# Dividing the softmax weights on GpSimd before the product with the values, one core

## The reference

```python
q, k, v = split(shift_token(x) @ wqkv)          # 128 -> 3 * 512
q, k = l2norm(q) * qs, l2norm(k) * ksc          # per head
q, k = rotary_xpos(q, k)
sim  = einsum('bhwid,bhwjd->bhwij', q * 8, look_around(k))   # own window and the one before
attn = softmax(where(mask, -max, sim))
out  = einsum('bhwij,bhwjd->bhwid', attn, look_around(v))
x    = x + out @ wo
x    = x + (a * gelu(g)) @ w2 + b2              # a, g from layernorm(shift_token(x)) @ w1
```

## Time and profile before

| | |
|---|---|
| median of 3 runs | 974.99 us (973.52 to 976.41) |
| the profiled execution | 971.3 us, of which the profiled span is 969.5 us |
| PE busy | 862.3 us (89%) |
| ACT busy | 701.7 us (72%) |
| DVE busy | 634.5 us (65%) |
| POOL busy | 631.0 us (65%) |
| mean granted PE clock | 0.983 of full speed |

### The profile page before, as it was taken

How to read it: one execution, slowest core, us unless ns; L and a number is a source line. 1 busy time by engine, 2 the same in 40 slices (tenths; PEclk the granted TensorE clock), 3 DMA queues, 4 the chain that set the end, 5 groups by cost and what they waited for, 6 DMA issues and landing times.

```text
span 969.5 us, 26414 instructions
## 1 busy us (share of the span) xinstructions
PE 862.3 (89%) x10836; PEld 580.5 (60%) x10836; DVE 634.5 (65%) x1082; ACT 701.7 (72%) x1449; POOL 631.0 (65%) x500
## 2 busy tenths in 40 slices
PE   0678889989899898998999989999999999999876
PEld 0345666666667666666566656565656565656552
DVE  5874666666667567576575776757575758575632
ACT  0446786977868779677797778787878787878651
POOL 4588677675876758667586665757575758585700
PEclk9979999999999999999999999999999999999997
DMA  9100000000000000000000000000000000000000
GB/s 295 30 1 3 1 2 2 3 3 2 2 3 1 3 1 1 3 2 3 1 2 3 1 2 2 1 21 4 17 7 23 2 23 2 21 3 24 1 23 11
DMA packets 20482, 13.47 MB, mean 14 GB/s; under 512 B 4579, under 2 KB 19597, under 8 KB 20237
## 3 DMA queue, kind: packets, MB, share of 16 engines
q1 hardware_dynamic: 15108, 10.49, 3.6%
q10 hardware_dynamic: 5256, 1.31, 0.7%
HBM read 9.70 MB, written 2.10 MB: 12 GB/s over the span
## 4 chain that ended last, share of the span: by engine, by line
PE 63%; ACT 15%; DVE 10%; issue 7%; POOL 3%; DMA 1%; DVEq 0%; POOLq 0%; SPq 0%; ACTq 0%
PE pQK L1181 8%; PE pS L1108 6%; PE pT L1093 5%; PE pT L1050 5%; PE pM L1125 5%; PE pV L1146 4%; PE pS L1082 4%; PE pM L1254 4%; DVE m L734 4%; PE pT L1237 3%; PE pQK L1345 3%; PE pM L1119 2%; PE pS L1069 2%; ACT prT L545 2%; ACT pr L598 1%
## 5 line engine op out<-in xcount | busy, mean ns | idle before, releaser
L366 POOL TENSOR_TENSOR rn<-rn,half_neg 128x16 f32<-128x16 f32 x64 | 187.5, 2929 | 5.3
L379 POOL TENSOR_TENSOR m<-m 128x1024 f32<-128x1024 f32 x64 | 150.9, 2358 | 0.0
L364 POOL TENSOR_SCALAR rn<-ss 128x16 f32<-128x16 f32 x64 | 16.3, 254 | 193.3 <-DVE ss L747 192.1
L386 POOL TENSOR_TENSOR qkn<-m,rn 128x1024 f32<-128x1024 f32 x64 | 121.7, 1902 | 5.0
L1181 PE MATMUL pQK<-wqkv,hT 128*128 128x512 f32 x256 | 123.6, 606 | 0.9 <-DVE m L734 0.9
L780 DVE TENSOR_REDUCE mx<-pS 128x8 f32<-128x1024 f32 x64 | 78.1, 1220 | 63.8 <-PE pS L1082 63.8
L561 ACT ACTIVATE sq<-pQK 128x1024 f32<-128x1024 f32 x64 | 65.4, 1022 | 25.5 <-PE pQK L1181 25.4
L747 DVE TENSOR_REDUCE ss<-sq 128x16 f32<-128x1024 f32 x64 | 77.6, 1213 | 6.7 <-ACT sq L561 6.4
L782 DVE TENSOR_TENSOR pr<-pS,mx 128x1024 f32<-128x1024 f32 x64 | 78.4, 1225 | 2.2
L521 ACT ACTIVATE kT<-pT 128x512 f32<-128x512 f32 x64 | 38.0, 595 | 57.3 <-PE pT L1050 56.8
L545 ACT ACTIVATE prT<-pT 128x1024 f32<-128x1024 f32 x64 | 65.0, 1016 | 15.6 <-PE pT L1093 14.8
(11 more groups left out here) (169 smaller groups left out, 2015.9 us busy)
## 6 DMA issues: line engine op xcount, KB each, us to landing
x<-in_L_attn_x SPq DMA_DIRECT2D x4, 512.0 KB, 9.4
xs<-in_L_attn_x SPq DMA_DIRECT2D x8, 256.0 KB, 2.8
out<-aqkT SPq DMA_DIRECT2D x8, 256.0 KB, 2.2
wqkv<-in_L_ffn_wqkv SPq DMA_DIRECT2D x2, 768.0 KB, 9.8
tab<-in_k_tab SPq DMA_DIRECT2D x1, 1024.0 KB, 10.4
w<-in_L_ffn_w SPq DMA_DIRECT2D x2, 341.0 KB, 10.5
wo<-in_L_ffn_wo SPq DMA_DIRECT2D x2, 256.0 KB
cst<-in_k_cst ACTq DMA_DIRECT2D x1, 404.5 KB, 4.3
```

The source lines that it names most:

```text
L366: eng.tensor_tensor(rn[:, k % 2, :], rn[:, k % 2, :], half_neg[:, 0:2 * H], ALU.pow).then_inc(S["rn_done"], 1)
L379: eng.tensor_tensor(m1[:, k % 2, :], m1[:, k % 2, :], m2[:, :], ALU.add).then_inc(S["add_done"], 1)
L386: eng.tensor_tensor(qkn[:, k % 2, :].rearrange("p (h d) -> p h d", d=DH), m1[:, k % 2, :].rearrange("p (h d) -> p h d", d=DH), rn[:, k % 2 ...
```

## The change

Each row of `pr` is summed on DVE after the exponential (`dve_totals`, a reduction over 128 x 1024 elements and a reciprocal of 128 x 8), and POOL multiplies the whole of `pr` with the reciprocals (`pool_weights`, 128 x 1024 elements). PE waits for that before it transposes the weights. `pe_values` then swaps its operands: the values are the stationary side and the transposed weights move, so that the output comes out already transposed, in `pS` for batch 0 and in `pM` for the others, and ACT evicts it directly to `oT`. The transposes of `o`, `dve_output` and the columns of ones are gone. `pe_values` of a batch runs one slot later than before (batch 0 at the end of slot 3). ACT's two carry copies become two DMAs a slot on SP's queue (`sp_carry`), with `vmix` in two buffers. `act_exp` moves ahead of the square. `qkn` becomes the same buffer as `m1`, `sm` moves to the buffer of `gg`, and the last transposes of a tile move from `pM` to `pV`.

```diff
+        def sp_carry(sp, step, b):
+            n, ct = count(step, b), step_count(step)
+            if not is_start(step):
+                need(sp, carried[b], 16 * (ct - 1))
+                sp.wait_ge(LS["s_mm"], n - 3)
+                sp.dma_start(kT[b][:, :, P:P + WIN], kT[b][:, :, WIN:P]).then_inc(carried[b], 16)
+            need(sp, kept[b], 16 * ct)
+            need(sp, LS["o_mm"], n - 3)
+            sp.wait_ge(LS["v_ev"], 2 * n + 2)
+            sp.dma_start(vmix[(ct + 1) % 2][b][64:P, :, :], vown[b][64:P, :, :]).then_inc(kept[b], 16)
...
                 pool_retention_norm(eng, new[1], 0)
                 return
+            turned = at(new, old, k - 2)
+            if turned:
+                pool_weights(eng, turned[1], turned[2])
             if old and k == NB - 1:
                 pool_ln(eng, old)
...
+        def pool_weights(eng, b, n):
+            eng.wait_ge(LS["rec_done"], n + 1)
+            eng.tensor_tensor(pr[:, b % 2, :, :], pr[:, b % 2, :, :],
+                              rec[:, b % 2, :].unsqueeze(2).broadcast_to([P, H, P]), ALU.mult).then_inc(LS["pn_done"], 1)
...
                 pool_mask_qk(eng, t, b)
                 if b + 2 < NB:
                     pool_retention_norm(eng, t, b + 2)
+            pool_weights(eng, 1, count((0, t), 1))
             if old:
                 pool_ln(eng, old)
...
+            if old and k > 0:
+                act_output(eng, old, k)
             if new:
-                if not is_start(new):
-                    need(eng, S["o_mm"], n - 3)
-                    eng.activation(vmix[k][64:P, :, 0:DH], vown[k][64:P, :, 0:DH], ACT.Copy).then_inc(S["v_kept"], 1)
-                    eng.activation(kT[k][:, :, P:P + WIN], kT[k][:, :, WIN:P], ACT.Copy).then_inc(S["carried"], 1)
...
-            if k == 0 and turned:
+            if turned and not (k == NB - 1 and new and new[0] == 0):
                 act_exp(eng, b, m)
...
-            else:
-                if old and k == NB - 1:
-                    act_shift_residual(eng, old)
-                if k > 0 and turned:
-                    act_exp(eng, b, m)
+            elif old and k == NB - 1:
+                act_shift_residual(eng, old)
...
-        def dve_output(eng, n):
+        def dve_totals(eng, b, n):
             S = LS
-            po = pS[:, :].rearrange("p (g z) -> p g z", g=2)[:, :, 0:4 * (DH + 1)].rearrange("p g (h d) -> p g h d", h=4)
-            eng.wait_ge(S["o_mm"], n + 1)
-            eng.reciprocal(rec[:, :, :], po[:, :, :, DH]).then_inc(S["rec_done"], 1)
-            eng.wait_ge(S["rec_done"], n + 1)
-            eng.tensor_tensor(o[:, :].rearrange("p (c g d) -> p g c d", g=2, d=DH), po[:, :, :, 0:DH],
-                              rec[:, :, :].unsqueeze(3).broadcast_to([P, 2, 4, DH]), ALU.mult).then_inc(S["o_done"], 1)
+            eng.wait_ge(S["exp_done"], n + 1)
+            eng.tensor_reduce(tot[:, :], pr[:, b % 2, :, :], AX.X, ALU.add).then_inc(S["tot_done"], 1)
+            eng.wait_ge(S["tot_done"], n + 1)
+            need(eng, S["pn_done"], n - 1)
+            eng.reciprocal(rec[:, b % 2, :], tot[:, :]).then_inc(S["rec_done"], 1)
...
             if k > 0 and old and not retain:
                 dve_residual(eng, old, k)
-            weighted = at(new, old, k - 3)
+            if turned and not retain:
+                dve_totals(eng, turned[1], turned[2])
...
                 if k + 2 < NB:
                     dve_retention_qk(eng, t, k + 2)
+                if k == 1:
+                    dve_totals(eng, 1, count((0, t), 1))
...
         def pe_turn_weights(eng, b, n, turned):
             S = LS
-            eng.wait_ge(S["exp_done"], n + 1)
+            eng.wait_ge(S["pn_done"], n + 1)
...
-            for i in range(H):
-                g, j = i // 4, i % 4
+            keys = (vmix[step_count(step) % 2][b], vown[b])
+            for j in range(4):
                 for w in range(2):
-                    col0 = g * 512 + j * (DH + 1)
-                    mm = eng.matmul(pS[64 * w:64 * w + 64, col0:col0 + DH + 1], prT[:, i, 64 * w:64 * w + 64],
-                                    (vown if w else vmix)[b][:, 2 * j + g, :], start=(j == 0), stop=True,
-                                    skip_group_check=True)
+                    for g in range(2):
+                        mm = eng.matmul(pooled(b)[64 * g:64 * g + 64, j * P + 64 * w:j * P + 64 * w + 64],
+                                        keys[w][:, 2 * j + g, :], prT[:, 4 * g + j, 64 * w:64 * w + 64],
+                                        start=True, stop=True, skip_group_check=True)
             mm.then_inc(S["o_mm"], 1)
...
+            if old and k > 0:
+                pe_values(eng, old, k, count(old, k), ff)
             if new:
                 l, n = new[0], count(new, k)
                 eng.wait_ge(S["h_ready"], 2 * n + 2)
                 need(eng, S["v_ev"], 2 * n)
+                if k == 2 and block_ffn:
+                    eng.wait_ge(G["osb"], ff[1] + 1)
...
-                pe_turn_output(eng, count(old, k))
+                pe_wo(eng, old[0], count(old, k))
...
-                    pe_ffn_out(eng, ff, lambda: weighted and pe_values(eng, weighted[1], weighted[2], turned))
+                    pe_ffn_out(eng, ff, first_wo)
...
+            if k == NB - 1 and new:
+                pe_values(eng, new, 0, count(new, 0))
```

More of the change, by code:

```diff
@@ L167, in program @@
         kT = [sb(f"kT{b}", [P, 4, P + WIN]) for b in range(NB)]
-        vown = [sb(f"vown{b}", [P, H, DH + 1]) for b in range(NB)]
-        vmix = [sb(f"vmix{b}", [P, H, DH + 1]) for b in range(NB)]
+        vown = [sb(f"vown{b}", [P, H, DH]) for b in range(NB)]
+        vmix = [[sb(f"vmix{u}_{b}", [P, H, DH]) for b in range(NB)] for u in range(2)]
         mx = sb("mx", [P, H])
@@ L318, in _, with body @@
                 sp.dma_start(w2[0:CHUNKS[2][1], l, 2, :], a["L0_ffn_w2"][l, 2 * P:HID, :]).then_inc(w_ld, 16)
[L320 to L327, removed]
+            def body(new, old, ff):
+                last = ff and ff[0] == 1
+                if last:
+                    need(sp, G["out"], 16 * ff[1])
+                    sp.dma_start(xs[:, :, :], x_steps[ff[1]]).then_inc(G["xs"], 16)
+                for k in range(NB):
+                    if new:
+                        sp_carry(sp, new, k)
+                if last:
+                    sp.wait_ge(G["osb"], ff[1] + 1)
+                    sp.dma_start(out_steps[ff[1]], osb[:, :, :]).then_inc(G["out"], 16)
+            run_bodies(sp, body)
+            for b in range(NB):
+                sp.wait_ge(kept[b], 16 * 2 * NT)
+                sp.wait_ge(carried[b], 16 * (2 * NT - 1))
             sp.wait_ge(G["out"], 16 * NT)
@@ L515, in act_slot @@
             turned = at(new, old, k - 2)
+            if old and k == 0 and old[0] == 1:
+                act_output(eng, old, 0)
             if turned:
@@ L533, in act_slot @@
                 eng.wait_ge(S["v_mm"], n + 1)
-                if not is_start(new):
-                    eng.wait_ge(S["v_kept"], n - 3)
+                need(eng, kept[k], 16 * step_count(new))
                 values = pV[:, :].rearrange("p (h d) -> p h d", h=H)
-                eng.activation(vown[k][:, :, 0:DH], values, ACT.Copy).then_inc(S["v_ev"], 1)
-                eng.activation(vmix[k][0:64, :, 0:DH], values[0:64], ACT.Copy).then_inc(S["v_ev"], 1)
+                eng.activation(vown[k][:, :, :], values, ACT.Copy).then_inc(S["v_ev"], 1)
+                eng.activation(vmix[step_count(new) % 2][k][0:64, :, :], values[0:64], ACT.Copy).then_inc(S["v_ev"], 1)
             if k == 1 and block_tile(ff) is not None:
@@ L600, in act_output @@
         def act_output(eng, step, b):
[L602 to L605, removed]
+            n = count(step, b)
+            eng.wait_ge(LS["o_mm"], n + 1)
+            need(eng, LS["wo_mm"], n)
+            eng.activation(oT[:, :, :], pooled(b)[:, 0:512].rearrange("p (c n) -> p c n", c=4),
+                           ACT.Copy).then_inc(LS["ot_ev"], 1)
         def act_gelu(eng, step, k):
@@ L765, in dve_rotate @@
             sum_squares()
-            if weighted:
-                dve_output(eng, weighted[2])
+            if final is not None:
+                dve_final(eng, final)
             if k == NB - 1 and l == 1 and normed:
@@ L823, in dve_slot @@
                 dve_hidden(eng, ff, 2)
-                if weighted:
-                    dve_output(eng, weighted[2])
                 dve_ffn_out(eng, ff)
             elif new:
-                dve_rotate(eng, new, k, weighted, normed=old)
-            elif weighted:
-                dve_output(eng, weighted[2])
+                dve_rotate(eng, new, k, normed=old, final=final)
+            elif final is not None:
+                dve_final(eng, final)
             if k == 0 and old:
@@ L1055, in pe_scores @@
             S = LS
-            evicted, subtracted, weighed = (counted(eng, v) for v in (2 * n + 2, n, n - 1))
             eng.wait_ge(mask_done, 1)
```

(10 more changed lines are left out.)

100 lines of the change are left out of this document (44 added, 56 removed).

## The result

The changed kernel takes 1015.55 us (median of four runs, 1013.55 to 1028.14) against 974.47 us for the kernel before on the same chip: ratio 1.0446, 95% interval 1.036 to 1.0532. The profiled execution took 1013.55 us (span 1011.7), 42.2 us more than before, where the sum of the prediction had 31.6. The spread of 15 us is new as well; the longest run had the lowest granted TensorE clock (0.953; the other three 0.965 to 0.972).

What follows compares the result with a forecast made beforehand. It took PE's transposes waiting for POOL's scaling two slots earlier as the loop that matters, POOL's longer round setting slots 1 to 3. Terms 21 + 3.2 + 3.2 + 2.2 + 2 = 31.6 on 971.3, plus 3.7: 1007 us, range 978 to 1035.

Steps and rivals of the forecast that it cites:

- PE and POOL as resources: Busy times expected in the changed profile: POOL near 753 us, PE near 834 us.
- POOL's multiplication, 1.90 us: New multiplication of 128 x 1024 by a broadcast operand in each slot, taken at 1.90 us, upper bound 2.36.
- Layer 0, slots 1 to 3, 18.65 us: From the start of slot 1, POOL's first round ends and slot 3 can start at 18.65 us; before, 16.35.
- that sign of being wrong: Prediction is wrong if DVE's new wait for the exponential makes PE's q and k projection wait for the rotation.
- PE ready for slot 3 at 15.5 us: Layer 0: with 7.75 us of work a slot, PE would be ready for slot 3 at 15.5 us after slot 1 starts.
- Retention, 2.9 us late and +1.3 us for the sum: Layer 0: PE enters the retention stretch 2.9 us late; DVE's uncovered sum for batch 1 adds 1.3 us.
- The rival that the lateness is taken up in the retention stretch: The 2.9 us are lost again among the retention stretch's waits: 987 us, 977 with the sum covered; 14%.
- The step of layer 0, +3.0 us: Layer 0 step: +2.9 lateness, +1.3 sum, -1.2 in slot 0, so +3.0 us, seven times: 21.
- The step of layer 1, +0.45 us: Layer 1 step: slot 3 waiting for POOL +0.85, layer-norm transposes +1.1, slot 0 -1.5, so +0.45 us, seven times: 3.2.
- The first steps and the drain: First step of layer 0 +3.2 us, first step of layer 1 +2.2 us, last batch in the drain +2 us.
- The whole: All terms over the whole kernel add up to 31.6 us more than the profiled execution before, 971.3 us.
- The carries, 0: 128 carries by DMA, issued about a slot ahead and due two slots (16 us) later, cost 0.

Runs made afterwards that it cites:

- a3_fill: Changed kernel with 20 transposes of a constant on PE ahead of its wait for POOL's scaling, in slot 3 only: 1005.74 us, 1.0343.
- b2_extra_wait: Kernel before with three idle POOL products (2.00 us together) at the new multiplication's place, waiting for the slot's exponential: 1003.31 us, 1.0329.
- b1_extra: Kernel before with three idle POOL products (2.00 us together) at the new multiplication's place, waiting for nothing: 981.77 us, 1.0104.
- a14_tiny_both: Changed kernel with POOL's multiplication cut to one column of 128 per head and DVE's sum taken over every eighth column: 983.6 us, 1.0119.
- a1_tiny: Changed kernel with POOL's multiplication cut to one column of 128 per head, its waits kept: 999.43 us, 1.0271.
- a8_fill_tot: Changed kernel with the edits of a2_totmove and a3_fill together: 996.6 us, 1.0244.
- a2_totmove: Changed kernel with DVE's sum for batch 1 in the retention stretch moved one piece later: 1007.07 us, 1.0367.
- c1_dma: Kernel before with only the two carries made by DMA on SP's queue, single value buffer kept: 965.46 us, 0.9936.
- a5_actcarry: Changed kernel with both carries made by ACT copies again instead of DMAs: 1022.78 us, 1.0525.
- a9_tiny_order: a1_tiny with, in slots 1 to 3, DVE's sum behind the sum of squares and POOL's short multiplication behind its maximum and power: 1022.01 us, 1.0522.

## Why the prediction was right, and where its sizes were off

The direction, the cause and the range held; the time came out 8.6 us above the 1007 us. By its own steps (the lengths of steps are taken from one POOL round of slot 1 to the next):

- *PE and POOL as resources.* POOL 749.4 us against my 753 held. PE had 847.3 against 834, because it works at half clock for longer: in a3_fill it is busy 869.0 us, of which the added transposes are 16 times 2.35, which leaves some 831 (an estimate).
- *POOL's multiplication, 1.90 us.* Measured 1.90. By the Trainium skill (GPSIMD Engine Reference, section 3.1) a two-input addition of 2048 fp32 elements measured 4497 ns on this engine; half of that, 2.25 us, is an estimate for 1024. It is near the addition here, 2.36 us, and not this form.
- *Layer 0, slots 1 to 3, 18.65 us.* Measured 19.06. The start of the maximum was 4.44 into the slot instead of 4.10, the multiplication 9.58 instead of 9.2; rounds without idleness came as said, and the wait of 3.21 us for POOL's scaling too. PE waited 2.3 us in the whole run for the rotation ahead of the q and k projection (0.9 before), so that sign of being wrong did not appear. b2_extra_wait shows the mechanism made alone, b1_extra that load is its smaller part.
- *PE ready for slot 3 at 15.5 us.* This would need slots of 7.75 us. PE's pieces of slot 1 in a14_tiny_both add up to 8.0 us without a gap, because the product with the values took 1.15 us (said 1.08) and the projection of v 1.05 (0.86 before), so that more than half of the 0.44 us of transposes that went came back. The maxima of a1_tiny are 8.3 us apart. None of this entered the sum, as POOL was later still, but it is why the short multiplication gave back only 17 us.
- *Retention, 2.9 us late and +1.3 us for the sum.* DVE's first product came at 29.6 us (said 29.1). In a3_fill PE's first retention product is 335.50 - 305.14 = 30.4 us after the start of slot 1, 3.5 us later than before, and the rest of the step is 0.4 us shorter, where the sum had +0.1: two small misses that cancel. The sum on DVE, 8 times 1.3 = 10 us, measured 9.6 with the clock held up (a3_fill against a8_fill_tot) and 7.7 without. The rival that the lateness is taken up in the retention stretch fell, as the step is longer by 3.0 us.
- *The step of layer 0, +3.0 us.* Measured +4.25, and +3.0 in a3_fill. The sum had no term for the clock and none for the pauses that the profile calls issue.
- *The step of layer 1, +0.45 us.* Measured +1.1, with no window below full clock there. Slot 1 to slot 3 took 20.8 us (said 20.35, and 19.5 before), and the transposes for the layer norm came another 1.5 us later in slot 3 (said 1.1). Over the seven steps this term was some 4.6 us too small.
- *The first steps and the drain.* The first step of layer 0 is longer by 5.9 us (said 3.2), the first of layer 1 shorter by 1.1 (said 2.2 longer), and what follows the last reading, at 931 us, is shorter by 1.1, drain included (said 2 longer for the drain).
- *The whole.* At a nearly full clock, in a3_fill, the span is 34.4 us longer than before, near the 31.6 of the sum. That is in part luck: the seven steps of layer 0 fit (21.2 against 21), but the misses in layer 1 and in the first step of layer 0, 5 and 3.5 us, are offset by those in the first step of layer 1 and the drain. The filling gave back 10 us (a3_fill against the changed kernel) and 12 us (a8_fill_tot against a2_totmove), clock and pauses together.
- *The carries, 0.* They are 124, not 128. No key eviction waited for a DMA; c1_dma shows that in the kernel before they are a gain. That 0 was right for the changed kernel, as far as a5_actcarry can tell.

What stays open: of the 1.2% that a14_tiny_both still loses, I name as likely that the product with the values and `wo` stand ahead of the projection of q and k on PE, from POOL's wait at 370.71 and the chain ahead of it, but no run undid this order by itself, nor the swapped operands of `pe_values`. Nor do the runs show why the clock falls in some steps and not in others with a gap of the same kind; the spread of the run times goes with it.

## What to carry to other kernels

Before giving a less busy engine more work, read in its timeline where its idle time lies and what the instructions queued behind the new one feed: 2 us without a wait cost 1.0% here, the same 2 us behind a wait 3.3%. An in-order queue makes everything behind the waiting instruction inherit its wait. Before turning an order round, follow what the moved instruction feeds back to itself: a9_tiny_order closed a new loop and lost 23 us. And where a change gives the matmul engine a new gap of a few microseconds, put a term for the granted clock into the sum, and look at its windows right behind the gap.

## What the hardware showed that I had not expected

- A gap of some 3 us on PE in slot 3 of a step was followed, in some steps, by windows of 4 or 5 us at a granted clock of 0.50 to 0.85, with PE full; in others, as after a gap of the same 3.21 us that ended at 195 us, it was not. Twenty transposes of a constant (0.27 us each by their pipelined length) in the gap took most of these stretches away: five windows of 4 us below full clock instead of 20, eleven of which lie in the first 136 us. The kernel became 10 us faster, not all of it by the clock.
- 124 copies of 128 KB within the on-chip memory, most of the 51908 packets of their queue, landed in 2.2 to 2.3 us each (medians of the two kinds), and no engine waited for one in the trace of the changed kernel.
- Multiplying by a broadcast operand took POOL 1.90 us and an addition of two full operands 2.36 us at the same 128x1024 elements.
